# Low-rank product of a feed-forward layer in tiles of TensorE's array

## What is computed

```python
h = take(table, ids)
x = layernorm(h)
f, i = sigmoid(x @ Wf.T), sigmoid(x @ Wi.T)
c = x @ Wh.T;  g = where(c >= 0, c + 0.5, sigmoid(c))
s[t] = f[t] * s[t-1] + i[t] * g[t]          # s[-1] = 0.5, per sequence
h = h + s
x = layernorm(h)
z = x @ ternary(w_fc).T + gate * (x @ v.T @ fast_b.T @ u.T)   # 256 -> 1024, rank 16
h = h + square(maximum(z, 0)) @ ternary(w_proj).T             # 1024 -> 256
```

## Time and profile before

| | us |
|---|---|
| median of 3 runs | 927.44 |
| lowest and highest | 926.73, 927.53 |
| the profiled execution, its own time | 927.5 |
| its span in the trace | 925.7 |
| busy: PE, DVE, ACT, POOL | 892.1, 748.0, 778.2, 463.6 |

### The profile page before, as it was taken

How to read it: one execution, slowest core, us unless ns; L and a number is a source line. 1 busy time by engine, 2 the same in 40 slices (tenths; PEclk the granted TensorE clock), 3 DMA queues, 4 the chain that set the end, 5 groups by cost and what they waited for, 6 DMA issues and landing times.

```text
span 925.7 us, 17445 instructions
## 1 busy us (share of the span) xinstructions
PE 892.1 (96%) x5177; PEld 511.9 (55%) x5177; DVE 748.0 (81%) x1316; ACT 778.2 (84%) x1156; POOL 463.6 (50%) x457
## 2 busy tenths in 40 slices
PE   3889999999999999999999999999999999999997
PEld 2335555555555565555555555555555555555654
DVE  6789888788888878888887888887888888788765
ACT  4578888888998888898888899888889988888884
POOL 6545554556545546655455665544665555533110
PEclk9989999999999999999999999999999999999999
DMA  4223335332332332333333233233223333332311
GB/s 143 46 50 63 84 77 93 98 76 68 87 82 74 97 96 59 79 84 78 85 96 81 63 85 82 74 96 96 64 78 87 77 80 96 94 59 73 79 44 46
DMA packets 227482, 73.38 MB, mean 79 GB/s; under 512 B 202246, under 2 KB 222288, under 8 KB 227456
## 3 DMA queue, kind: packets, MB, share of 16 engines
q1 hardware_dynamic: 221312, 68.86, 31.1%
q0 software_dynamic: 6144, 4.21, 2.0%
HBM read 27.68 MB, written 24.64 MB: 57 GB/s over the span
## 4 chain that ended last, share of the span: by engine, by line
PE 92%; DVE 2%; ACT 2%; issue 2%; POOL 1%; DMA 0%; SPq 0%; ACTq 0%; POOLq 0%; DVEq 0%
PE bank L799 35%; PE y_ps L736 23%; PE bank L838 23%; PE bank L842 6%; PE bank L722 3%; PE turned L767 2%; ACT normed L484 1%; ACT sq L551 0%; DMA w_raw<-wh 0%; ACT relu L538 0%; POOL rows_raw L387 0%; PE turned L692 0%; DVE stats L914 0%; DVE sq_lo L1098 0%; DVE y_sb L1106 0%
## 5 line engine op out<-in xcount | busy, mean ns | idle before, releaser
L838 PE MATMUL bank<-x_cols,fc_t 128*128 128x512 f16 x1024 | 264.0, 380 | 0.0
L397 POOL TENSOR_SCALAR var_eps<-moments 128x4 f32<-128x4 f32 x64 | 59.7, 933 | 354.8 <-DVE moments L918 354.8
L799 PE MATMUL bank<-x_cols,w_hi 128*128 128x512 f16 x768 | 229.8, 381 | 4.6 <-ACT cand_lin L527 3.0
L799 PE MATMUL bank<-x_cols,w_lo 128*128 128x512 f16 x768 | 229.8, 381 | 0.0
L736 PE MATMUL y_ps<-proj_t,sq_hi 128*128 128x256 bf16 x1024 | 225.6, 273 | 1.1 <-DVE sq_lo L1098 1.1
L736 PE MATMUL y_ps<-proj_t,sq_lo 128*128 128x256 bf16 x1024 | 225.6, 273 | 0.0
L387 POOL DMA_INDIRECT rows_raw<-table,idx_now x128 | 161.4, 1261 | 60.2 <-issue 31.0
L538 ACT ACTIVATE relu<-bank,relu_scale 128x512 f32<-128x512 f32 x256 | 165.9, 691 | 13.7 <-PE bank L842 13.7
L838 PEld LDWEIGHTS bank<-x_cols,fc_t 128*128 128x128 bf16 x1024 | 100.6, 98 | 114.4 <-issue 1.6
L1098 DVE TENSOR_TENSOR sq_lo<-sq,sq_hi 128x1024 f16<-128x1024 f32 x128 | 150.5, 1214 | 4.4 <-ACT sq L551 4.3
L484 ACT ACTIVATE normed<-h,shift,rstd 128x256 f32<-128x256 f32 x256 | 133.0, 608 | 8.6 <-POOL shift L405 8.6
(11 more groups left out here) (132 smaller groups left out, 935.6 us busy)
## 6 DMA issues: line engine op xcount, KB each, us to landing
out<-out_sb SPq DMA_DIRECT2D x31, 512.0 KB, 2.9
spill<-hid_blocks SPq DMA_DIRECT2D x30, 256.0 KB, 2.2
hid_rows<-spill SPq DMA_DIRECT2D x120, 64.0 KB
rows_raw<-table,idx_now POOLq DMA_INDIRECT x128, 2.9
x_cols<-x_rows SPq DMA_TRANSPOSE x122, 2.8
sq<-w_fc SPq DMA_DIRECT2D x1, 1024.0 KB, 6.1
pj_raw<-w_proj SPq DMA_DIRECT2D x1, 1024.0 KB
out<-out_sb SPq DMA_DIRECT2D x2, 256.0 KB, 2.1
```

Source lines behind the costliest of these rows:

```text
L799: ins = pe.matmul(bank[gate_bank[p]][:, :], w[:, k, q, :], x_part(0, par, part)[:, :, k, :], start=(k == 0 and w is w_hi and part == 0), s ...
L838: pe.matmul(dst[:, :], fc_t[:, f, k, :], x_part(1, 0, part)[:, :, k, :], start=(k == 0 and part == 0), stop=False)
```

## The change

The low-rank product is split by array tiles. `low_a` becomes 32 columns (16 high, 16 low). `low_parts` runs four matmuls, for both halves of the channels and both parts of x, each into its own 32 partitions of one bank (`low_ps`, the second half of `turned`). ACT copies this bank in f32 to `parts` (`copy_parts`). `low_sums` is one f32 matmul with the 0/1 matrix `spread`, which adds the eight groups of 16 rows and repeats the sum eight times. ACT makes `low_hi` of it (`low_high`), DVE `low_lo` (`low_low`), both with 128 partitions. `narrow` multiplies `low_u` with them in matmuls of 32 rows, for four wide blocks at a time: four with `low_hi`, four with `low_lo`. `opened` says how many of the four blocks have had their wide matmuls before; the others are started by `narrow` and ended by `wide(f, False)`.

Banks alternate with the parity of the step, and since the low rank no longer needs one of the four, blocks 2 and 3 wait for gates 4 and 5. The transposes of `hid` (`turn_upper`) go to the first half of `turned`. ACT evicts three gates of the second half before `low_high` and clips four blocks before it squares. DVE does `x_low(0)` before `low_low` and `emit` after the scan. In steps 1, 2 and 32 `low_sums` stands between the wide blocks 1 and 2, and `narrow(0, 4)` after block 3. DVE builds `spread` once from `ident`.

```diff
-        low_a = sb("low_a", [P, KD, P], F16)
+        low_a = sb("low_a", [P, KD, 2, R], F16)
+        spread_one = sb("spread_one", [P, R])
+        spread = sb("spread", [P, P])
...
-        low = sb("low", [P, CHUNK], F16)
+        parts = sb("parts", [P, CHUNK])
+        low_hi = sb("low_hi", [P, CHUNK], F16)
+        low_lo = sb("low_lo", [P, CHUNK], F16)
...
-        gate_bank = (0, 1, 2, 3, 1, 2)
-        fc_bank = (3, 0, 1, 2, 3, 0, 1, 2)
+        low_ps = turned[:, CHUNK:2 * CHUNK]
+        turned_half = turned[:, 0:CHUNK].rearrange("p (j d) -> p j d", j=TILES)
...
+        def gate_bank(p, par):
+            return bank[(p + 2 * par) % 4]
+        def fc_bank(f, par):
+            return bank[(f + 2 + 2 * par) % 4]
...
+            def copy_parts(m):
+                act.wait_ge(part_done, m + 1)
+                wait(act, low_done, m)
+                act.activation(parts[:, :], low_ps, ACT.Copy).then_inc(parts_ready, 1)
...
             def low_high(m):
                 act.wait_ge(low_done, m + 1)
                 wait(act, fc_done, FC * m)
-                act.activation(low[:, :], bank[0][:, :], ACT.Copy).then_inc(low_hi_ready, 1)
-
...
+            def evict(n, par, e, q, dst, func, bias=0.0):
...
@@ -559,20 +581,18 @@
                 ahead = known_below(n, N - 1)
                 def back(n):
-                    clip(m, 0)
-                    clip(m, 1)
+                    for f in range(4):
+                        clip(m, f, par)
                     if front:
                         square_high(m, 0)
                     square(m, 0)
-                    clip(m, 2)
-                    clip(m, 3)
-                    clip(m, 4)
+                    clip(m, 4, par)
+                    clip(m, 5, par)
                     if front:
                         square_high(m, 1)
-                    clip(m, 5)
                     square(m, 1)
-                    clip(m, 6)
-                    clip(m, 7)
+                    clip(m, 6, par)
+                    clip(m, 7, par)
                     if front:
                         square_high(m, 2)
                     square(m, 2)
...
+                copy_parts(m)
+                if front:
+                    evict(n, par, 1, 1, inp, ACT.Sigmoid)
+                    evict(n, par, 1, 2, cand_sig, ACT.Sigmoid)
                 low_high(m)
                 if front:
-                    evict(n, 1, 2, cand_sig, ACT.Sigmoid)
-                    evict(n, 1, 3, cand_lin, ACT.Identity, 0.5)
+                    evict(n, par, 1, 3, cand_lin, ACT.Identity, 0.5)
...
-            def low_rank(n, m, front):
+            def low_parts(n, m):
                 if isinstance(n, int) and n == 1:
                     pe.wait_ge(cols_lo[1], 2)
-                    pe.wait_ge(low_a_ready, 1)
+                    pe.wait_ge(low_a_ready, 2)
                 elif isinstance(n, int) and n == N:
                     pe.wait_ge(cols_lo[1], 4)
                 else:
                     pe.wait_ge(x_landed[1], 32 * m)
-                if front:
-                    pe.wait_ge(gate_taken, 8 * n + 4)
-                else:
-                    pe.wait_ge(relu_ready, FC * (n - 2) + 6)
+                    pe.wait_ge(low_lo_ready, m)
+                if isinstance(n, int) and n == 2:
+                    pe.wait_ge(h1_ready, 2)
                 for k in range(KD):
                     for part in range(2):
-                        ins = pe.matmul(bank[0][:, :], low_a[:, k, :], x_part(1, 0, part)[:, :, k, :],
-                                        start=(k == 0 and part == 0), stop=(k == KD - 1 and part == 1))
-                ins.then_inc(low_done, 1)
+                        at = slice(BLOCK * (2 * k + part), BLOCK * (2 * k + part + 1))
+                        ins = pe.matmul(low_ps[at, :], low_a[:, k, :, :].rearrange("p a r -> p (a r)"),
+                                        x_part(1, 0, part)[:, :, k, :], start=True, stop=True)
+                ins.then_inc(part_done, 1)
+            def low_sums(m):
+                if isinstance(m, int) and m == 0:
+                    pe.wait_ge(spread_ready, 1)
+                pe.wait_ge(parts_ready, m + 1)
+                pe.matmul(low_ps, spread[:, :], parts[:, :], start=True, stop=True).then_inc(low_done, 1)
...
+            def turn_upper(c):
+                pe.wait_ge(scanned, 4 * (c + 1))
+                wait(pe, h1_ready, c)
+                for j in range(TILES):
+                    ins = pe.transpose(turned_half[:, j, :], hid[:, 1, j * P:(j + 1) * P], ident[:, :])
+                ins.then_inc(hid_turned, 1)
...
+                def gate(p):
+                    e, g = divmod(p, 3)
+                    if p < 4:
+                        wait(pe, relu_ready, FC * (n - 2) + 5 + p)
+                        if first:
+                            pe.wait_ge(gate_taken, 8)
+                    else:
+                        pe.wait_ge(gate_taken, 8 * n + (4, 4 if start else 3)[p - 4])
+                    q = 2 * g + e
...
+                def free(f):
+                    if f > 3:
+                        pe.wait_ge(relu_ready, FC * m + f - 3)
+                    elif front:
+                        pe.wait_ge(gate_taken, 8 * n + (2, 5, 6, 8)[f])
+                    else:
+                        pe.wait_ge(relu_ready, FC * (n - 2) + (7, 8, 5, 6)[f])
+                def wide(f, opens):
+                    if opens:
+                        free(f)
+                    if first:
+                        pe.wait_ge(fc_landed[f // 4], 16)
+                    for k in range(KD):
+                        for part in range(2):
+                            ins = pe.matmul(fc_bank(f, par)[:, :], fc_t[:, f, k, :], x_part(1, 0, part)[:, :, k, :],
+                                            start=(opens and k == 0 and part == 0),
+                                            stop=(not opens and k == KD - 1 and part == 1))
+                    if not opens:
+                        ins.then_inc(fc_done, 1)
+                def narrow(first_f, opened):
+                    for f in range(first_f + opened, first_f + 4):
+                        free(f)
+                    for part, ready in ((low_hi, low_hi_ready), (low_lo, low_lo_ready)):
+                        pe.wait_ge(ready, m + 1)
+                        for i in range(4):
+                            f, at = first_f + i, slice(BLOCK * i, BLOCK * (i + 1))
+                            ins = pe.matmul(fc_bank(f, par)[:, :], low_u[at, f * P:(f + 1) * P], part[at, :],
+                                            start=(part is low_hi and i >= opened),
+                                            stop=(part is low_lo and i < opened))
+                            if part is low_lo and i < opened:
+                                ins.then_inc(fc_done, 1)
                 if front:
                     if start:
                         pe.wait_ge(cols_lo[0], 2)
                         pe.wait_ge(w_lo_ready, 3)
                     else:
...
+                    for p in range(3):
+                        gate(p)
+                    if first:
+                        turn_hidden(0)
+                    if steady:
+                        project(n - 2)
+                    gate(3)
+                    gate(4)
+                    if steady:
+                        low_parts(n, m)
+                    gate(5)
+                    if start:
+                        return
+                    if steady:
+                        low_sums(m)
+                if not steady or not front:
+                    if first:
+                        turn_normed(1)
+                    else:
+                        project(n - 2)
+                    low_parts(n, m)
...
+                wide(0, True)
+                wide(1, True)
+                if steady and front:
+                    narrow(0, 2)
+                    wide(2, False)
+                    wide(3, False)
+                else:
+                    low_sums(m)
+                    wide(2, True)
+                    wide(3, True)
+                    narrow(0, 4)
+                wide(4, True)
+                if front and not first:
+                    turn_upper(n)
+                wide(5, True)
+                narrow(4, 2)
+                wide(6, False)
+                if first:
+                    turn_hidden(1)
+                wide(7, False)
...
                 a_cols = y_ps[:, 2, 64:64 + KD * R].rearrange("p (k r) -> p k r", k=KD)
                 mark(dve.tensor_copy(a_hi[:, :, :], a_cols))
                 settle()
+                dve.tensor_copy(low_a[:, :, 0, :], a_hi[:, :, :]).then_inc(low_a_ready, 1)
+                dve.tensor_tensor(low_a[:, :, 1, :], a_cols, a_hi[:, :, :], ALU.subtract).then_inc(low_a_ready, 1)
...
+            dve.wait_ge(ident_ready, 1)
+            mark(dve.tensor_reduce(spread_one[:, :], ident[:, :].rearrange("p (c r) -> p r c", r=R), AX, ALU.add))
+            settle()
```

(17 more changed lines are left out.)

134 lines of the change are left out of this document (39 added, 95 removed).

## The result

The changed kernel takes 934.36 us (median of 4 runs, 932.87 to 936.09) against 927.12 for the kernel before on the same chip: 1.0079 times as long, 95% interval 1.0063 to 1.0095. It is slower by 0.8%, where 921.6 us and a gain of 0.6% were forecast. The time lies inside the range of 911 to 945, the sign is wrong. The profiled execution took 932.87 us, 931.1 of it span, against 927.5 and 925.7. It is the fastest of its four, 1.5 us under their median, so the spans differ by 5.4 us where the medians differ by 7.2; the traces can divide only the 5.4.

The account below looks back on a forecast made before the run. PE was taken to bound the loop: 2.59 - 0.22 - 0.86 - 0.86 - 0.36 = 0.29 us less a step, 8.4 over 29 steps, ends +2.5: 927.5 - 8.4 + 2.5 = 921.6 us, range 911 to 945.

Parts of the forecast that it names:

- The bound: In the loop nothing makes PE wait, busy 28.00 of 28.00 us; PE's pitches count, not durations.
- Side by side: Tiled matmuls run side by side: four `low_parts` in one pitch, 0.22 us; two `narrow` 0.86 us a step.
- rivals 2 and 4: Rival 2: weight loads pace `narrow`, 1.57 for 0.86, chance 0.12; rival 4: tiles not side by side, 1005 us, chance 0.06.
- The f32 sum: `low_sums`, one f32 matmul of 512 columns, takes two passes, 0.86 us a step.
- The change of shape: Into and out of `low_parts` and each `narrow`, six times a step: 0.06 us each, 0.36 a step.
- Rival 1: The pipe empties at each change of shape, 0.164 us each, six a step: 939.6 us, slower; chance 0.20.
- My own point of decision: Price per change of shape at which rival 1 decides: 0.11 us in the loop, 0.09 with the ends counted.
- ACT and DVE in the loop: Their added work and chain are covered: margins 0.2 to 0.3 us at `narrow`, 0.2 at `turn_upper`; cost nothing to 0.1.
- rival 3: Low-rank chain through ACT and DVE makes PE wait 0.3 us a step at `narrow` and `turn_upper`: 930.3 us; chance 0.12.
- The ends: Start before the loop and last step together cost 2.5 us more.
- The last step: Stall of 1.65 us goes, first clip moves to about 908.9; DVE ends 1.2 to 1.6 us later.
- The signs to watch for: Prediction wrong if the step is over 27.4 us or the ends cost over 5; right if about 27.0.

Follow-up runs that it names:

- two others: Changed kernel with DVE's `x_low(0)` back behind `low_low`: 951.49 us; changed kernel with ACT's squares of blocks 0 and 1 back between clips 1 and 2: 959.43 us.
- the moves: Changed kernel, steps 1 and 2: ACT's normalise and x_high before `low_high`, x_high before `copy_parts`, DVE's output scales before `low_low`; 933.07 us; with f16 sum 919.50.
- the f16 sum: Changed kernel with partial sums copied as f16 high (ACT) and low (DVE) parts, added by two f16 matmuls in place of one f32: 922.09 us.
- the earlier sum: Kernel with f16 sum and the moves, sum put before the first wide block in steps 1, 2, 32, some ACT and DVE orders of step 1 changed: 918.55 us.
- the earlier `parts_lo`: Kernel with f16 sum and the earlier sum, DVE's low part of the partial sums moved ahead of three small scale operations in step 1: 917.62 us.

## Why the prediction was wrong, point by point

- **The bound.** Right: PE before and after, with no wait in the loop. Only its pitches counted.
- **Side by side** (0.22 for four `low_parts`, 0.86 for the two `narrow`; rivals 2 and 4). Right: four records in 0.40, the next four 0.22 later, so 0.43 for eight, and the four tiles' loads within 0.10. Neither rival came. No row of before had a tiled matmul, so this was argued and not read. Part 3 of TensorE: Matmul & The Clock Gate in the Trainium skill gives 3.07 times for four row tiles; from start to start these rows show 4, as a tiled group costs one pitch, like any matmul in a stream. What spoils the factor here stands at its edges.
- **The f32 sum,** 0.86. Right to the hundredth: 451.78 - 450.92. Two passes, as the earlier trace rows had it.
- **The change of shape,** 0.06. This is the step that failed. I took it nearer to the f16 to f32 change of the earlier trace rows, which costs nothing, than to the emptied pipe of 0.164. The runs show 0.10, in six places of the step and in three of the experiments' new places. A step's sum becomes 2.59 - (0.43 + 0.86 + 2 x 0.64) = 0.02 in place of 0.29, 0.6 us over 29 steps for 8.4; the trace shows 0.0. This term alone turned the sign: with the loop's 8.4 us gained and the ends as they came, 5.2, the kernel would have been 3.2 us faster. Rival 1 had the right direction, but its price of 0.164 was too high, and its 939.6 us by 5. My own point of decision stood at 0.09 with the ends: between my value and the rival's, and I gave a single value between two bounds that lay on either side of it. Like the tiles themselves, the change of shape had no row of before, so the sign hung on a guess. The Trainium skill (TensorEngine Tiling, Key Properties) says that a change of tiling mode drains the engine. The rows agree that something is given up, and show how much: 0.10, not the full 0.164. Whether the 0.10 is part of a drain or a weight load that is no longer hidden (0.09 to 0.10 long, starting together with its matmul) no run separates.
- **ACT and DVE in the loop** (rival 3). Right, with more cover than reckoned: `low_lo` 0.35 before it is wanted, the scan 0.55 before `turn_upper`. Dearer changes of shape lengthened the cover, as said there, so part of it is the luck of the mis-sized term. That the orders are needed, which I argued from "about 1 us" for `emit`, was tried for two others: 0.6 and 0.75 a step. The move of `emit` itself was not tried.
- **The ends,** +2.5. Mis-sized: 5.2. The last step is right, 1.3 for 1.2 to 1.6. The start cost 3.9 for 1.1. I had the later clips (3.0 us, for 2.3), but put the loss on gate 4 of step 2 alone, which waited 0.88 and not 2.6, and took the wait of 1.58 before the first `low_u` as saved: it went, and waits of 0.77 and 0.83 came in its place. Not seen were the place of `low_low` ahead of `relu_scale` on DVE, PE's own standstill of 2.35 us and the lower clock that followed, which cost 1.5 us, and chunk 3's split of x behind `copy_parts`. How much the orders cost and how much the place of the sum isn't settled: in the traces the moves bring step 3 0.3 us forward in the changed kernel and 1.9 with the f16 sum, the earlier sum 1.1, the earlier `parts_lo` 1.7, each with a different length of the slow stretches in it.
- **The signs to watch for** named "over 5 for the ends" and "over 27.4 a step" as what would make the forecast wrong. The first came; the second limit was set too high, as 27.28 was enough.

What stays open: why the clock comes back when it does. In the kernels compared it returned to 1.00 from its first slow stretch between 62 and 66 us, with the mean from 60 to 80 us between 0.74 and 0.91, and no edit explains it. With it stays open how the rest of the start's 3.9 us divides.

## What to carry to other kernels

Count the changes of array shape beside the matmuls: in this kernel a tiled group pays only if what it saves exceeds 0.2 us, the price of going in and out, so gather same-shaped tiles in one group, as `narrow` does with eight in 0.43. Where splitting a product makes partial sums that have to be added, price that addition first: here the f32 matmul ate all that the tiles had saved, and the same sum in two f16 matmuls was half as dear. When one term has no row in the trace and its bounds lie on both sides of the break-even, the forecast's sign is that term's; measure it before, or say that the sign is open.

## What the runs showed of the hardware

- A change between full and tiled shape, in either direction, or between two tiled shapes costs 0.10 us: starts 0.31 to 0.33 apart for 0.216, all at 512 columns and f16. The weight load behind it isn't run ahead; it starts 0.30 after the last matmul and its own matmul 0.01 later.
- Four tiles of 32 rows at 512 columns take one pitch: the next four start 0.22 later. Four tiles of 32 columns take 0.43 with their two changes of 0.10, so 0.22 by themselves. Their four loads lie within 0.10.
- An f32 matmul of 512 columns costs 0.86, four f16 pitches; f16 high and low parts against 0/1 weights cost 0.43.
- A standstill of PE of 2.35 us early in the kernel (66.3 to 68.6) was followed by a granted clock of 0.50 from 69 to 72, and eight matmuls took 3.2 us for 1.73. Eight of the profiled executions have a standstill of 2.3 to 2.4 us there; in seven of them the clock fell behind it, in one (`narrow` with full matmuls, 2.29 us) it didn't, nor in the two where only 0.77 us of it were left.
